# Attention on Trainium2: values every step, projections in half pieces, row maxima's banks shared with the shifts, one addition moved to VectorE

## The reference, cut to what matters

```python
qkv = x @ qkv_w + qkv_b
q, k, v = jnp.moveaxis(qkv.reshape(b, n, 3, H, D), 2, 0)
attn = jax.nn.softmax(jnp.einsum('bnhd,bmhd->bhnm', q, k) * scale, axis=-1)
out = jnp.einsum('bhnm,bmhd->bnhd', attn, v).reshape(b, n, c) @ proj_w + proj_b
x = _layernorm(x + out, axis=-1)
```

## Time and profile before

| what | value |
|---|---|
| median of 3 runs | 3656.3 us (3652.07 to 3658.67) |
| span of the profiled execution | 3644.6 us (11.7 us under the median; no other time of that execution is recorded) |
| self-attention with chunks 0 to 31 | from about 100 to 2173 us |
| four chunks (one unit) in the middle | 259.5 us |
| last three periods before the final chunk | 194.2 us |

### The profile page before, as it was taken

One profiled execution on the slowest core, in us unless ns is written; L12 is line 12 of the kernel. 1 busy time (PEld: TensorE's weight loads), 2 busy tenths in 40 slices (PEclk: granted clock), 3 DMA queues, 4 the chain that ended last, 5 costly groups with the idle time before them and its releaser, 6 DMA issues. The chain is left out here.

```text
span 3644.6 us, 50074 instructions
## 1 busy us (share of the span) xinstructions
PE 3423.0 (94%) x18021; PEld 2227.0 (61%) x18021; DVE 2510.0 (69%) x4512; ACT 1672.6 (46%) x3043; POOL 1995.2 (55%) x1008
## 2 busy tenths in 40 slices
PE   7999999999999999999999987999959899999996
PEld 5545455455455555455454435877739789988885
DVE  5777777777777777777777735889834765566667
ACT  2455555555555555555555553444312333233332
POOL 2688888888888888888898950011110101110112
PEclk9999999999999999999999998999969999999998
DMA  6322221321312312213120022132132333323332
GB/s 223 103 56 65 86 62 62 93 67 61 97 50 73 97 50 85 73 50 106 56 64 24 15 93 66 58 121 81 53 119 81 113 113 104 116 89 114 117 128 99
DMA packets 190278, 308.49 MB, mean 85 GB/s; under 512 B 25514, under 2 KB 72234, under 8 KB 190011
## 3 DMA queue, kind: packets, MB, share of 16 engines
q1 hardware_dynamic: 166970, 243.82, 21.8%
q0 software_dynamic: 14592, 44.32, 3.5%
q10 hardware_dynamic: 8448, 16.78, 1.3%
HBM read 195.66 MB, written 61.33 MB: 71 GB/s over the span
## 5 line engine op out<-in xcount | busy, mean ns | idle before, releaser
L511 DVE TENSOR_REDUCE sa_part_max<-sa_mx 128x1 f32<-128x512 f32 x2048 | 1282.4, 680 | 539.8 <-PE sa_mx L625 536.0
L466 ACT ACTIVATE sa_prob<-sa_sc 128x512 f32<-128x512 f32 x2010 | 1101.3, 595 | 803.7 <-PE sa_sc L692 764.4
L268 POOL TENSOR_TENSOR sa_quad_sum<-sa_quad_sum,sa_prob 128x1024 f32<-128x1024 f32 x500 | 1174.6, 2382 | 6.3 <-ACT sa_prob L466 6.3
L268 POOL TENSOR_TENSOR sa_quad_sum<-sa_prob 128x1024 f32<-128x1024 f32 x250 | 588.2, 2372 | 266.9 <-ACT sa_prob L466 266.9
L2055 PE MATMUL ex_h<-ex_xT,ex_w 128*128 128x384 f32 (+2 forms) x2688 | 463.9, 328 | 52.0 <-issue 24.4
L625 PE MATMUL sa_mx<-sa_k_even,sa_q_stack 96*128 96x512 f32 x1024 | 490.8, 483 | 17.2 <-DVE sa_part_max L511 7.5
L625 PE MATMUL sa_mx<-sa_k_odd,sa_q_stack 96*128 96x512 f32 x1024 | 476.6, 465 | 10.0 <-DVE sa_part_max L511 8.6
L2055 PEld LDWEIGHTS ex_h<-ex_xT,ex_w 128*128 128x128 f32 x2688 | 445.3, 194 | 64.8 <-issue 32.6
L692 PE MATMUL sa_sc<-sa_q_stack,sa_k_even 98*128 98x512 f32 x1024 | 427.1, 417 | 0.0
L2066 PE MATMUL ex_acc<-ex_w,ex_hT 128*128 128x512 f32 x1719 | 415.6, 392 | 1.9 <-DVE ex_hT L1994 1.6
L692 PE MATMUL sa_sc<-sa_q_stack,sa_k_odd 98*128 98x512 f32 x986 | 415.5, 423 | 1.6 <-ACT sa_prob L466 1.6
(11 more groups left out here) (229 smaller groups left out, 3776.8 us busy)
## 6 DMA issues: line engine op xcount, KB each, us to landing
ex_w_in<-in_L_ffn_w_dram SPq DMA_DIRECT2D x130, 512.0 KB, 4.1
sa_xT<-xT SPq DMA_DIRECT2D x57, 1024.0 KB, 5.1
sa_q_stack<-sa_hilo SPq DMA_DIRECT2D x372, 64.0 KB, 2.0
rows<-sa_empty SPq DMA_DIRECT2D x48, 257.0 KB, 3.7
ex_rows<-rows POOLq DMA_DIRECT2D x8, 1542.0 KB, 7.7
sa_k_odd<-sa_hilo SPq DMA_DIRECT2D x192, 64.0 KB, 2.0
ex_xg<-rows POOLq DMA_DIRECT2D x48, 256.0 KB
sa_k_even<-sa_hilo SPq DMA_DIRECT2D x168, 64.0 KB, 2.0
```

The costliest lines, as they stand in the source:

```text
L268: pool.tensor_tensor(quad_sum[:, i % 2, heads, :], so_far, prob[:, k, heads, :], ALU.add).then_inc(quad_ready, 1)
L466: act.activation(prob[:, kt % 4, j, :], score_bank(n)[:, :], ACT.Exp, scale=SCALE).then_inc(prob_ready, 1)
L511: dve.reduce_max(part_max[:, q, j, k:k + 1], mx[n % 3][:, :], AX_X).then_inc(max_read, 1)
```

## The change

- `burst` runs in every step, with the values of one step (`add_values(step - 1)`) in place of two steps in every second one.
- Each of a projection's four parts is cut in two halves (256 columns of q or k, two of the four inner matmuls of v). `PLACES` puts the eight halves at the ends of steps 0, 0, 1, 2, 2, 3, 4, 4 of a job's five; the jobs start at steps 0, 5 and 10 and are left at (5, 1), (10, 1) and (15, 1), in place of steps 4, 8 and 12.
- The shifts are transposed into the next of the three maxima banks in turn (`max_turn`, `shift_turn`, `turn_over`), and copied out after the reduction of (13, 3) in place of (14, 0). `misc` is the projections' alone.
- One of the six additions, the first one of heads 2 and 3 (k = 1, half = 1), is `add_pair` on VectorE, at step 2 of each four, after head 1. GpSimd's second addition of that half waits for it.
- SyncE issues `shift_rows` at step 15, ahead of that step's job.

```diff
-    QUADS, ADDS = T // 4, 6
+    QUADS, ADDS = T // 4, 5
+    PAIR_AT = (2, 1)
-    PARTS_AT = ((0, 1, 2, 3), (4, 5, 6, 7), (8, 9, 10, 11))
+    END, HALVES = HG - 1, 2
+    PLACES = [[(5 * i + kt, END) for kt in (0, 0, 1, 2, 2, 3, 4, 4)] for i in range(3)]
+    LEFT_AT = ((5, 1), (10, 1), (15, 1))
...
             for half in range(2):
+                if by_vector(d, k, half):
+                    continue
                 heads = slice(2 * half, 2 * half + 2)
                 pool.wait_ge(prob_ready, (g * T + 4 * i + k) * HG + 2 * half + 2)
                 if k > 1:
-                    pool.wait_ge(quad_ready, d * ADDS + 2 * (k - 1) - 1 + half)
+                    added(pool, d, k - 1, half)
...
+        def add_pair(d):
+
+            after(dve, den_mm, d - 1)
+            dve.wait_ge(prob_ready, (4 * d + 2) * HG)
+            dve.tensor_tensor(quad_sum[:, d % 2, 2:4, :], prob[:, 0, 2:4, :], prob[:, 1, 2:4, :], ALU.add).then_inc(pair_ready, 1)
...
-                    if i == 1 and (g, kt) in LEAVE_AT:
-                        leave_psum(LEAVE_AT[g, kt])
+                    if (g, kt, i) in LEAVE_AT:
+                        leave_psum(LEAVE_AT[g, kt, i])
+                    if (kt % 4, i) == PAIR_AT:
+                        add_pair(g * QUADS + kt // 4)
                     if (kt, i) in INVERT_AT and g > 0:
                         invert(g - 1, INVERT_AT.index((kt, i)))
...
                 weight = wq[:, part, :] if job.what == "q" else wkv[:, part, 0, :]
-                last = pe.matmul(bank[:, :], weight, xT[:, slot, part, :], start=(part == 0), stop=(part == KC - 1))
+                cols = slice(half * BANK // HALVES, (half + 1) * BANK // HALVES)
+                last = pe.matmul(bank[:, cols], weight, xT[:, slot, part, cols],
+                                 start=(part == 0 and half == 0), stop=(part == KC - 1 and half == HALVES - 1), skip_group_check=True)
...
             if step > 0:
-                add_values(step - 2)
                 add_values(step - 1)
...
-                        if i == 1 and kt % 2 == 0:
+                        if i == 1:
                             burst(g, kt)
...
+    def max_turn(n):
+
+        return n + max(n - SHIFT_AT, 0) // NMAX
+
+    def shift_turn(g):
+        return max_turn((g + 1) * NMAX + SHIFT_AT) - 1
```

More of the change, by code:

```diff
@@ L121, in self_attention @@
     FIRST_OPS = [i for i in ALONE + sum(BETWEEN, []) if i[0] != "t"]
-    Job = namedtuple("Job", "unit what n chunk load place")
-    JOBS = [Job(0, what, n, None, None, None) for what, n in FIRST_OPS]
-    JOBS += [Job(u + o.ahead, o.what, o.n, u * NQ + o.c, u * len(LOADS) + o.load, PARTS_AT[i % 3])
+    Job = namedtuple("Job", "unit what n chunk load place left_at")
+    JOBS = [Job(0, what, n, None, None, None, None) for what, n in FIRST_OPS]
+    JOBS += [Job(u + o.ahead, o.what, o.n, u * NQ + o.c, u * len(LOADS) + o.load, PLACES[i % 3], LEFT_AT[i % 3])
              for u in range(UNITS) for i, o in enumerate(OPS) if u + o.ahead < UNITS]
@@ L129, in self_attention @@
     VALUES = [i for i, job in enumerate(JOBS) if job.what == "v"]
-    PART_AT = {(job.chunk, kt): (i, part) for i, job in enumerate(JOBS) if job.place for part, kt in enumerate(job.place)}
-    LEAVE_AT = {(job.chunk, job.place[-1] + 1): i for i, job in enumerate(JOBS) if job.place}
+    PARTS_AT = {}
+    for i, job in enumerate(JOBS):
+        for part, at in enumerate(job.place or ()):
+            PARTS_AT.setdefault((job.chunk, *at), []).append((i, part))
+    LEAVE_AT = {(job.chunk, *job.left_at): i for i, job in enumerate(JOBS) if job.place}
     USERS = {}
@@ L349, in _ @@
                     empty_slots(g - 4)
-                if (g, kt) not in LEAVE_AT:
+                if kt == T - 1:
+                    shift_rows(g + 1)
+                leaves = [LEAVE_AT[g, kt, i] for i in range(PER_STEP) if (g, kt, i) in LEAVE_AT]
+                if not leaves:
                     continue
-                i = LEAVE_AT[g, kt]
+                i = leaves[0]
                 job = JOBS[i]
@@ L591, in project_part @@
             job = JOBS[i]
+            part, half = divmod(part, HALVES)
             first = job.place is None
@@ L594, in project_part @@
             slot = job.n % 2 if first else job.load % 2
-            if part == 0:
+            if part == 0 and half == 0:
                 if job.what == "q":
@@ L603, in project_part @@
                     after(pe, in_x[slot], 16 * loads_until(job.load))
-                if not first and i == 0 or not first and JOBS[i - 1].chunk != job.chunk:
-                    pe.wait_ge(shiftT_ready, job.chunk + 1)
-                elif not first or i >= 3:
+                if not first or i >= 3:
                     before = i - 3 if first else i - 1
@@ L644, in row_sums @@
         def row_sums(d):
-            pe.wait_ge(quad_ready, (d + 1) * ADDS)
+            added(pe, d, 3, 1)
             for j in range(HG):
@@ L693, in score, with project_first @@
                       q_stack[0:AUG, j, g % NQ * BANK:(g % NQ + 1) * BANK], start=True, stop=True).then_inc(sc_mm, 1)
+        def project_first(i, part):
+            for half in range(HALVES):
+                project_part(i, part * HALVES + half)
         pe.wait_ge(ident_ready, 1)
@@ L700, in _ @@
                 else:
-                    project_part(FIRST_OPS.index((what, n)), part)
+                    project_first(FIRST_OPS.index((what, n)), part)
         stacked_first(pe, "q", 0)
@@ L740, in chunk @@
                         last_burst(kt)
-                    if i == 2 and kt == T - EARLY and g + 1 < CHUNKS:
+                    if i == SHIFT_AT - 1 and kt == T - EARLY and g + 1 < CHUNKS:
                         transpose_shift(g + 1)
-                if (g, kt) in PART_AT:
-                    project_part(*PART_AT[g, kt])
+                    for job, part in PARTS_AT.get((g, kt, i), ()):
+                        project_part(job, part)
         for g in range(LAST):
```

53 lines of the change are left out of this document (35 added, 18 removed).

## The result

| | before | changed |
|---|---|---|
| median (range) of 8 runs each | 3652.03 us (3648.96 to 3658.67) | 3660.91 us (3657.98 to 3663.34) |
| ratio, 95% interval | | 1.0023 [1.0014, 1.0031] |
| span of the profiled execution | 3644.6 us | 3661.6 us |

The change makes the kernel slower by 0.23%, 8.9 us. I had the direction; I forecast 26 us and 3682 us.

What follows compares the result with a forecast made beforehand. TensorE was taken as the bound, 94% real work. Terms summed to 264.6 us against 259.5 per four chunks, 36 us over 28 chunks, less 10 in the last unit: +26 on 3656.3, 3682 us, range 3625 to 3740.

Steps and rivals of the forecast that it cites:

- the sum of the changed kernel's work: TensorE's work over four chunks without new waits: 243.1 us before, plus 10.9 for bursts and 0.8 for projection halves.
- the base: Starting point for the difference: 259.5 us per four chunks between transposes, and 3656.3 us for the whole kernel before.
- the last unit: Final chunks, nearly without projections: the last three periods fall from 194.2 to 183.5 us, giving back 10.
- the shifts' bank: Shifts transposed into a maxima bank: the copy out comes one reduction earlier, so no cost was expected.
- the pair rows of four at step 15: Step 15 has no projection piece, so four pairs run in a row: 0.2 to 0.3 us a chunk, 1.2 per four.
- the take-out in step 5: Four reciprocals stand ahead of VectorE's take-out, so TensorE waits 0.9 us in three of four chunks: 2.6.
- the held addition: In step 10 GpSimd's addition starts first and holds VectorE's: TensorE waits 0.9 us a chunk, 3.6 per four.
- the stacked q: In a unit's third and fourth chunk q's DMAs land late for step 13: 0.3 us each, 0.6 per four chunks.
- waits won and bursts paid: Bursts in every step, per four chunks: about 11 us of ScalarE's waits go, 10.9 us of column-group gaps are added.
- Rival 2: VectorE's addition is late in every group, 0.9 us four times a chunk: 3750 us; chance 0.15.
- rival 1: VectorE always finds GpSimd idle, held time under 0.6 us a chunk: 3644 us, or 3622 with take-outs and moves in time; chance 0.28.
- Rival 3: Gains and costs cancel, the second burst's gaps lying inside ScalarE waits that stay: 3656 us; chance 0.12.

Runs made afterwards that it cites:

- burst_alone: The kernel before with bursts of one step's values in every step, nothing else changed; no difference in the timed runs, 0.25 us more a chunk.
- six_adds: The changed kernel with all six additions on GpSimd, none on VectorE; the first 28 chunks take 1826.7 us against 1842.7.
- shift_first: The changed kernel with VectorE copying the shifts out ahead of the reduction of (13, 3); step 14 takes 4.81 us in place of 5.30.
- halves_alone: The kernel before with each q or k projection part issued as two matmuls of 256 columns; 64.99 us a chunk against 65.02.
- double_bursts: The changed kernel with bursts of two steps' values in every second step again; 0.56 us a chunk slower than the changed kernel.
- before_again: The kernel before, unchanged, profiled a second time; the changed kernel's stage is 8.5 us longer than in this profile, 12.8 than in the first.
- no_add_at_10: The changed kernel with all six additions on GpSimd in step 10's group, except in the last unit; a chunk wins 0.67 us.
- combined kernel: The changed kernel with shifts copied out first, reciprocals at steps 3, 4, 7, 8, and step 10's addition on GpSimd except in the last unit; 3613.18 us, 0.9890 of before.

## Why the prediction was right in its steps and wrong in its size

In short: the sizes of the waits were near; the step that carries the miss is the sum of the changed kernel's work, 254.8 us for four chunks where 253.0 is measured, with the base and the last unit beside it; and one step was wrong in its mechanism, the "Nothing" for the shifts' bank, which costs 0.51 us a chunk.

**Right, by place.** Per four chunks, forecast against the step table: the pair rows of four at step 15 with step 0 1.2 and 1.2; the take-out in step 5 2.6 and 3.1; the held addition 3.6 and 3.1; the stacked q 0.6 and 0.6 (steps 12 and 13; but only 0.3 of it stands in the third and fourth chunk of a unit, where the q is waited for, so the match is half luck). The addition starts in steps 2 and 6 at 1.40 and 1.41, forecast 1.4, and is 1.22 long, forecast 1.2. The 0.9 of the held addition is two errors that nearly cancel: GpSimd's start at 1.56 and its 2.38 us give 3.94, not 4.2, and the trace has VectorE held until 3.97 and the bank free at 5.71 (944.11 - 938.40), not 6.1; TensorE wants it at 5.02 (the first score of step 11 at 4.78, and half a pair), not 5.25. burst_alone shows that waits won and bursts paid cancel, as 10.9 against about 11 said. Rival 2 fell (nothing is held in steps 2 and 6 of the first 28 chunks; in the last unit step 6 of two chunks is), rival 1 too (0.77 held a chunk, above its 0.6). Rival 3's 3656 is the nearest number, but its mechanism is not there: a burst costs its full 1.20 in the steps of 3.07 (four pairs are 1.87).

**Right in size, wrong in cause: step 14.** I gave 1.8 to an addition held there and nothing to the shifts' bank. It is 2.0, and that the sum came out near is luck, for all of it is the bank: the addition is never held in step 14, six_adds keeps the loss, shift_first takes it away. The step that failed is "The copy out comes one reduction earlier ... Nothing": a reduction earlier on VectorE, but the third maxima matmul behind the transposes (954.09, 954.88, 955.93) wants that bank, where before it was the next chunk's first job that wanted `misc`.

**The term that was mis-sized: the work of the changed kernel.** I built it from parts, 243.1 + 10.9 + 0.8 = 254.8 for four chunks; it is 4 x 63.24 = 253.0. Of the 1.8 the halves are 0.8 (halves_alone: nothing), and the rest is small errors a piece: 0.47 for 0.4675 in 256 pairs is 0.6, 0.87 for 0.86 in 48 parts 0.5, 0.88 for 0.86 in 16 row sums 0.3 and 0.40 for 0.36 in four transposes 0.2, less 0.6 for 64 bursts at 1.20 that I had at 1.19. The waits came to 10.3 where I had 9.8, and the base was 259.9 (4 x 64.98), not the 259.5 of the one period that I read. So 3.4 in place of 5.1, 24 in place of 36 us for 28 chunks. A difference of 2% between two sums of 250 cannot carry errors of 0.7% in either: what the waits lost should have been set against what they won, and the work only where it differs. Over 28 chunks this term is 12.6 us of the 17 by which the forecast of +26 was too high; the base adds 2.8, the waits take off 3.5, and the last unit, below, is 5.8.

**Two more terms.** Against the second profile of before, chunks 28 to 30 gave back 12.4 (197.7 to 185.3) where I had 10, and chunk 31, which I left out, 3.4 (51.4 to 48.0). With 24.3 for the first 28 (1818.4 to 1842.7) that is 24.3 - 12.4 - 3.4 = 8.5, against 36 - 10 = 26. By the transposes, which the forecast went by, the last three periods gave back 6.9 (194.2 to 187.3) where it had 194.2 - 183.5 = 10.7, so that term was too high, and what made up for it lies behind the last transposes, which no term covered. Of chunk 31's 3.4, 2.4 are the granted clock (below) and 1.0 the single bursts: burst_alone has 48.0 there, the first profile of before 49.0, both at full clock.

**The base.** I laid the difference on the median of three, 3656.3; the eight runs have 3652.0, which is 4 of the 21 us by which 3682 missed. The one profile that I had was a quick execution, by 4.3 us in the stage alone. Of these, 2.4 are chunk 31's, where the granted clock differed (below); the rest stays open.

**Where the expected gain went.** It did not lie off the path: about 2.5 us of ScalarE's waits a chunk were won, and paid back in the gaps of eight more bursts. The loss is on VectorE, at three places of 0.5 to 0.8 us, each shown by an edit of its own: in step 14 it is the order of its queue alone, in step 5 the order for two thirds, and in step 11 the moved addition beside the take-out.

## What to carry to other kernels

When work moves to an engine that is 70% busy, read its queue for the instruction behind each added one, and for the next use of the bank that it frees: two of the three losses here went or shrank by a new order alone, the third only by giving one addition in four back to GpSimd, and together that turned 0.2% slower into 1.1% faster. Price a change by the parts that differ, not by two sums over everything. And compare like stretches of several profiles, with the granted clock of each stretch beside its time, so that what differs from execution to execution, or by the clock, is not taken for a wait: double_bursts is 0.56 us a chunk slower, and at full clock it is not slower at all.

## What the runs showed of the hardware

**The hold goes both ways.** No row of before showed whether a wide VectorE addition delays GpSimd. Timeline of the changed kernel, step 2:

```profile
972.86 1.22 DVE L559 TENSOR_TENSOR sa_quad_sum<-sa_prob 128x1024 f32<-128x1024 f32 x1
```

```profile
973.05 3.27 POOL L308 TENSOR_TENSOR sa_quad_sum<-sa_quad_sum,sa_prob 128x1024 f32<-128x1024 f32 x1 [1.03 <-ACT sa_prob L508]
```

GpSimd's addition starts 0.19 after VectorE's and takes 3.27 where 2.38 is its time: 0.9 longer, until 2.24 after VectorE's end. In step 10 VectorE's took 2.20 behind GpSimd's. This is what the Trainium skill states in "SBUF — State Buffer", section "SBUF: two separate sides": the one that starts first keeps the shared ports for its whole instruction. The trace agrees, with 0.9 and 1.0 us.

**The granted clock in the last unit.** Windows of 2100 to 2120 and 2120 to 2140 us, the first profile of before and then before_again (TensorE, weight loads, VectorE, ScalarE, GpSimd, granted clock, DMA):

```profile
2100.00:2120.00 20.00, 15.93 (x70) 6.13 (x69) 11.31 (x14) 8.80 (x16) 17.19 (x8) 0.83 0.02 3
2120.00:2140.00 20.00, 17.56 (x98) 6.85 (x98) 5.29 (x9) 15.60 (x31) 17.10 (x8) 1.00 0.98 300
```

```profile
2100.00:2120.00 20.00, 15.92 (x71) 6.17 (x66) 11.28 (x14) 8.83 (x16) 17.55 (x8) 0.78 0.01 2
2120.00:2140.00 20.00, 17.98 (x83) 6.05 (x76) 2.19 (x3) 12.09 (x23) 13.92 (x7) 0.80 0.91 272
```

In the kernel before, TensorE waits 3.4 us for the shift, and in both executions the granted clock is down in that window. From 2120 on the two part, though the kernel is the same; a burst of chunk 31 in before_again:

```profile
2126.62 3.64 PE L640 MATMUL sa_pv<-sa_prob,sa_v_odd 128*32 128x512 f32 x16
```

3.64 us is 1.9 times the 1.92 of the same sixteen at full clock: the lower of the two levels, 1.2 GHz. It goes with 2.4 us in chunk 31 (51.4 for 49.0 in the first profile, which is at full clock there). The changed kernel has a lower stretch 100 us earlier. Its chunks 28 to 30, and then those of no_add_at_10, whose instructions are the same from chunk 28 on:

```profile
1951.50:2136.80 185.30, 179.19 (x896) 83.27 (x895) 147.50 (x221) 109.11 (x199) 152.40 (x64) 0.97 0.06 17
```

```profile
1934.80:2117.40 182.60, 176.52 (x895) 81.92 (x896) 147.35 (x221) 108.99 (x199) 152.30 (x64) 0.99 0.06 18
```

The same instructions take 2.7 us less at 0.99 than at 0.97. In before_again these three chunks have 0.93, and in the combined kernel 1.00. So part of the gain in the last unit is the granted clock. An estimate of its most: 0.93 of 197.7 us is 14 us of full clock lost, 0.97 of 185.3 is 6, so at most 8 of the 12.4; how much of that is the change's, with its shorter waits, and how much differs from execution to execution, no run here separates.
